# Third stage, selective scan: the terms of a tile summed by two VectorE reductions along the terms' axis in place of seven GpSimd additions

## What is computed

```python
x_ssm = silu(causal_depthwise_conv(x_ssm, conv_w, conv_b))
dt = softplus(x_ssm @ dt_w + dt_b)
Bm = x_ssm @ B_w          # 16 states
Cm = x_ssm @ C_w
A = -exp(log_A)
# for each token t, in order:
h = h * exp(min(dt_t * A, 0)) + (dt_t * x_t) * B_t
y_t = sum over states (h * C_t)
# then
y = y + x_ssm * D_param
y = (y * silu(z)) @ W_out
out = residual + y
```

## Time and profile before

| | us |
|---|---|
| median of the 3 runs | 1027.2 |
| the three runs | 1036.17, 1026.03, 1027.2 |
| the profiled execution, time | 1038.13 |
| the profiled execution, span of the core | 1036.3 |
| VectorE busy | 679.9 (66%) |
| TensorE matmuls busy | 860.4 (83%) |
| GpSimd busy | 457.0 (44%) |
| first and last multiplication of line 1139 start at | 529.5, 735.8 |

### The profile page before, as it was taken

The page is one execution under the profiler, slowest core; times in us unless marked ns, Lnnn a source line. Parts: engine busy times, 40 slices in busy tenths (PEclk is TensorE's granted clock), DMA queues, the critical chain, the costliest instruction groups (busy, mean ns, idle before and its releaser), DMA issues. The chain is left out here.

```text
span 1036.3 us, 21603 instructions
## 1 busy us (share of the span) xinstructions
PE 860.4 (83%) x8256; PEld 709.6 (68%) x8256; DVE 679.9 (66%) x1965; ACT 556.8 (54%) x1050; POOL 457.0 (44%) x781
## 2 busy tenths in 40 slices
PE   1888882669999999988777778987479999999994
PEld 1778771558888888866645556765358878888783
DVE  2687765665888888764279999999864181461712
ACT  1454551236676766646567787787355263552630
POOL 1486754222454545336357777776740020020201
PEclk9985665557899999888888888788679999999997
DMA  9100001100000000000000000000000000000000
GB/s 310 49 19 17 22 18 44 49 1 2 1 3 2 2 2 2 1 2 1 1 1 1 1 1 1 1 1 1 0 1 1 1 14 8 1 21 1 14 8 20
DMA packets 22149, 16.76 MB, mean 16 GB/s; under 512 B 2576, under 2 KB 20376, under 8 KB 21792
## 3 DMA queue, kind: packets, MB, share of 16 engines
q1 hardware_dynamic: 17408, 8.39, 2.9%
q10 hardware_dynamic: 4640, 7.01, 2.0%
HBM read 11.20 MB, written 4.19 MB: 15 GB/s over the span
## 5 line engine op out<-in xcount | busy, mean ns | idle before, releaser
L118 POOL TENSOR_TENSOR d_ln_ve<-d_ln_mv,eps 128x4 f32<-128x4 f32 x16 | 3.2, 201 | 228.7 <-DVE d_ln_mv L112 228.7
L1331 PE MATMUL ps<-h_h,wh_h 128*128 128x512 f32 x256 | 99.6, 389 | 0.0
L1333 PE MATMUL ps<-h_l,wh_h 128*128 128x512 f32 x256 | 99.6, 389 | 0.0
L1332 PE MATMUL ps<-h_h,wh_l 128*128 128x512 f32 x256 | 99.6, 389 | 0.0
L1410 PE MATMUL ps<-w_e,he 128*128 128x128 f32 x512 | 88.0, 312 | 3.2 <-ACT he L684 2.9
L684 ACT ACTIVATE he<-ps,pp 128x256 f32<-128x256 f32 x128 | 59.8, 472 | 43.5 <-PE ps L1333 38.0
L1344 PEld LDWEIGHTS ps<-mov,hbd 32*128 32x128 f32 x2048 | 82.1, 242 | 0.0
L1410 PEld LDWEIGHTS ps<-w_e,he 128*128 128x128 f32 x512 | 78.1, 224 | 5.4 <-ACT he L684 4.7
L1344 PE MATMUL ps<-mov,hbd 32*128 32x32 f32 (+1 forms) x2048 | 80.7, 317 | 0.0
L1298 DVE TENSOR_TENSOR d_y<-ps,w_s 128x512 f32<-128x512 f32 x8 | 5.5, 692 | 102.9 <-PE ps L1729 102.9
L1264 DVE TENSOR_TENSOR h_l<-hid,h_h 128x512 fp32r<-128x512 f32 x64 | 48.5, 772 | 31.2 <-ACT h_h L891 30.3
(11 more groups left out here) (255 smaller groups left out, 2610.8 us busy)
## 6 DMA issues: line engine op xcount, KB each, us to landing
x<-in_x SPq DMA_DIRECT2D x16, 128.0 KB
w_h<-in_w_h ACTq DMA_DIRECT2D x2, 1024.0 KB, 8.3
x<-x SPq DMA_DIRECT2D x16, 128.0 KB, 1.8
xB<-x SPq DMA_DIRECT2D x32, 64.0 KB
out_x<-xB SPq DMA_DIRECT2D x32, 64.0 KB
w_m<-in_w_m ACTq DMA_DIRECT2D x3, 256.0 KB, 5.5
xB<-in_w_e ACTq DMA_DIRECT2D x1, 512.0 KB
w_e<-in_w_e ACTq DMA_DIRECT2D x1, 512.0 KB
```

The source lines that it names most:

```text
L1331: pe.matmul(dst, a_h, b_h, start=start, stop=True, skip_group_check=True)
L1332: pe.matmul(dst, a_l, b_h, start=False, stop=True, skip_group_check=True)
L1333: return pe.matmul(dst, a_h, b_l, start=False, stop=True, skip_group_check=True)
```

## The change

Two new tiles per lane stand beside `term`: `ysum`, 32 chunks x 8 tokens, and `late`, 32 x 4. In `terms`, VectorE now raises a new semaphore `c_terms` with the second multiplication, waits for it, and issues two reductions: the first adds the four wide terms of each of the 256 tokens into `ysum`, the second the four thin ones into `late`, and the second raises `c_term`. `sums` is gone from GpSimd. `skips` gets one more addition, linked to the next, of `late` to the last four tokens of each chunk in `ysum` (128 elements), then adds `xd` and raises `c_ys` as before. `add_sums` reads `ysum`. All terms of a token are added now, where `sums` left out those that are zero.

```diff
--- before.py
+++ after.py
@@ -289,6 +289,8 @@
         hd = sb("hd", [P, DS, NB])
         hc = [sb(f"hc{l}", [P, DS, NCH]) for l in LANES]
         term = [sb(f"term{l}", [P, HALF * NCH * (CH + HALF)]) for l in LANES]
+        ysum = [sb(f"ysum{l}", [P, NCH, CH]) for l in LANES]
+        late = [sb(f"late{l}", [P, NCH, HALF]) for l in LANES]
         cbd = [sb(f"cbd{l}", [P, NT]) for l in LANES]
         hcT = [sb(f"hcT{l}", [P, 4, D]) for l in LANES]
         xd, yi, ya = (chan("c_" + n) for n in ("xd", "yi", "ya"))
@@ -330,7 +332,7 @@
             a_y a_zn a_z a_o a_x a_stored b_xn b_xb b_t_ps b_qk_ps b_v_ps b_kT b_hbd b_vT b_vbd b_s_ps b_sm b_ex
             b_pT b_m_ps b_ctx b_ctxt_ps b_msgT b_y b_y_ps b_zn b_h b_ht_ps b_hT b_hTl b_l_ps b_lg b_le b_hot b_hott_ps b_hotT b_on b_z b_o
             b_x c_xn_ c_t_ps c_xT_ c_in_ps c_zs_ c_xs_ c_dt_ps c_b_ps c_c_ps c_zb_ c_sp_
-            c_dt_ c_dec c_bcT c_prod c_g1_ps c_term c_ys c_xd c_cbd c_wall c_wt_ps c_u c_yi1 c_bbd c_xr c_br_ps c_wendT c_st_ps
+            c_dt_ c_dec c_bcT c_prod c_g1_ps c_terms c_term c_ys c_xd c_cbd c_wall c_wt_ps c_u c_yi1 c_bbd c_xr c_br_ps c_wendT c_st_ps
             c_hs c_hct_ps c_hcT c_yi_ps c_y c_out_ps c_o_ c_x d_xn_ d_t_ps d_xh d_xl d_y_ps d_o_ d_x d_stored""".split()
         S = {n: sem(n) for n in SEMS}
         he_ps, he_ready, e_done = (sem(n) for n in ("he_ps", "he_ready", "e_done"))
@@ -540,23 +542,14 @@
                 pool.tensor_tensor(c_ln1.nm[m][:, :], c_ln1.nm[m][:, :], minus[:, 0:2], ALU.mult
                                    ).then_inc(c_ln1.rstd_ready, 1)
 
-            def sums(t):
-                l = t % 2
+            def skips(t):
+                l = t % 2
+                pool.wait_ge(S["c_xd"], t + 1)
                 pool.wait_ge(S["c_term"], t + 1)
-                wide = term[l][:, 0:HALF * PAIR].rearrange("p (s c t) -> p s c t", s=HALF, t=CH)
-                thin = term[l][:, HALF * PAIR:].rearrange("p (s c t) -> p s c t", s=HALF, t=HALF)
-                y = wide[:, HALF - 1]
-                for j in range(1, HALF):
-                    chain.link(pool.tensor_tensor(y[:, :, j:CH], y[:, :, j:CH], wide[:, HALF - 1 - j, :, j:CH], ALU.add))
-                for j in range(HALF, CH):
-                    chain.link(pool.tensor_tensor(y[:, :, j:CH], y[:, :, j:CH], thin[:, CH - 1 - j, :, j - HALF:HALF],
-                                                  ALU.add))
-
-            def skips(t):
-                l = t % 2
-                pool.wait_ge(S["c_xd"], t + 1)
-                y = term[l][:, (HALF - 1) * PAIR:HALF * PAIR]
-                pool.tensor_tensor(y, y, xd[l][:, :], ALU.add).then_inc(S["c_ys"], 1)
+                y = ysum[l][:, :, HALF:CH]
+                chain.link(pool.tensor_tensor(y, y, late[l][:, :, :], ALU.add))
+                pool.tensor_tensor(flat3(ysum[l][:, :, :]), flat3(ysum[l][:, :, :]), xd[l][:, :], ALU.add
+                                   ).then_inc(S["c_ys"], 1)
 
             def stored(t):
                 pool.wait_ge(S["c_o_"], t + 1)
@@ -569,8 +562,6 @@
                     products(1)
                 if have(-2):
                     c_ln2.rstd_and_shift(pool, chain, eps, half, minus, (n - 2) % 4, n - 1)
-                if have(0):
-                    sums(n)
                 if have(4):
                     scales(n + 4)
                 if have(0):
@@ -1142,13 +1133,19 @@
                 dve.tensor_tensor(split(term[l][:, HALF * PAIR:].rearrange("p (s c t) -> p s c t", s=HALF, t=HALF)),
                                   split(w[:, 0:HALF, :, HALF:CH]),
                                   ps[:, PAIRS:PAIRS + 4, WIDE:BC_AT].rearrange("p g (s c t) -> p s g c t", s=HALF, t=HALF),
-                                  ALU.mult).then_inc(S["c_term"], 1)
+                                  ALU.mult).then_inc(S["c_terms"], 1)
+                dve.wait_ge(S["c_terms"], t + 1)
+                dve.tensor_reduce(flat3(ysum[l][:, :, :]), term[l][:, 0:HALF * PAIR].rearrange("p (s k) -> p k s", s=HALF),
+                                  AX.X, ALU.add)
+                dve.tensor_reduce(late[l][:, :, :].rearrange("p c t -> p (c t)"),
+                                  term[l][:, HALF * PAIR:].rearrange("p (s k) -> p k s", s=HALF), AX.X, ALU.add
+                                  ).then_inc(S["c_term"], 1)
 
             def add_sums(t):
                 l = t % 2
                 dve.wait_ge(S["c_ys"], t + 1)
                 dve.wait_ge(S["c_yi1"], t + 1)
-                chain.link(dve.tensor_tensor(yi[l][:, :], yi[l][:, :], term[l][:, (HALF - 1) * PAIR:HALF * PAIR], ALU.add))
+                chain.link(dve.tensor_tensor(yi[l][:, :], yi[l][:, :], flat3(ysum[l][:, :, :]), ALU.add))
 
             def gated(t):
                 l = t % 2
```

More of the change, by code:

```diff
@@ L541, in scales @@
                                    ).then_inc(c_ln1.rstd_ready, 1)
-            def sums(t):
-                l = t % 2
-                pool.wait_ge(S["c_term"], t + 1)
-                wide = term[l][:, 0:HALF * PAIR].rearrange("p (s c t) -> p s c t", s=HALF, t=CH)
-                thin = term[l][:, HALF * PAIR:].rearrange("p (s c t) -> p s c t", s=HALF, t=HALF)
-                y = wide[:, HALF - 1]
-                for j in range(1, HALF):
-                    chain.link(pool.tensor_tensor(y[:, :, j:CH], y[:, :, j:CH], wide[:, HALF - 1 - j, :, j:CH], ALU.add))
-                for j in range(HALF, CH):
-                    chain.link(pool.tensor_tensor(y[:, :, j:CH], y[:, :, j:CH], thin[:, CH - 1 - j, :, j - HALF:HALF],
-                                                  ALU.add))
             def skips(t):
@@ L557, in skips @@
                 pool.wait_ge(S["c_xd"], t + 1)
-                y = term[l][:, (HALF - 1) * PAIR:HALF * PAIR]
-                pool.tensor_tensor(y, y, xd[l][:, :], ALU.add).then_inc(S["c_ys"], 1)
+                pool.wait_ge(S["c_term"], t + 1)
+                y = ysum[l][:, :, HALF:CH]
+                chain.link(pool.tensor_tensor(y, y, late[l][:, :, :], ALU.add))
+                pool.tensor_tensor(flat3(ysum[l][:, :, :]), flat3(ysum[l][:, :, :]), xd[l][:, :], ALU.add
+                                   ).then_inc(S["c_ys"], 1)
             def stored(t):
```

## The result

The changed kernel takes 1061.9 us in the median of four runs (1059.1 to 1065.2), the kernel before 1030.6 (1026.0 to 1036.2). The ratio is 1.030, 95% interval 1.023 to 1.037: slower by 3%, about 31 us. The forecast was 1062. The profiled execution after has a span of 1063.1 us against 1036.3.

What follows compares the result with a forecast made beforehand. VectorE's own program was taken to bound the third stage: 48.8 us of strided reductions less 13.7 us given back make +35.1 on a median of 1027.2, so 1062 us; own range 1058 to 1074, whole range 1040 to 1076.

Steps and rivals of the forecast that it cites:

- The bound: Third stage: its length is VectorE's own program, 13.86 us a tile, so work put on VectorE counts in full.
- The reductions: VectorE's two added reductions and the wait on c_terms in terms: 3.05 us a tile with the stride, 48.8 us over 16.
- the full-rate rival: VectorE's new reductions run at one element a cycle wherever they read: 1.84 us a tile, +15.7, 1042.9 us; chance 22%.
- The give-back: VectorE's operations on two SBUF tiles speed up once GpSimd's seven additions are gone: 13.7 us less.
- The half that I gave to lines 1194 and 1108: Less sure recovery of these two VectorE operations from GpSimd's work: 4.1 us counted of 8.2.
- the part that I called sure: Lines 1163 and 1172 on VectorE, slowed beside GpSimd's additions, return to their fastest times: 9.6 us.
- The sum: Whole change: 48.8 us added on VectorE less 13.7 us returned, +35.1 us, 1062 us for the median.
- What was taken to cost nothing: c_term coming 3.05 us later, before pairs on TensorE and skips on GpSimd, was to cost no time.
- The clock rival: TensorE idles more in longer turns, its granted clock falls to 0.50 and its chain holds up VectorE: +47, 1074; chance 6%.
- The "not slower" rival: Reductions at full rate and VectorE regaining 32.1 us from GpSimd, line 1118 included: -2.7, 1024.5 us; chance 6%.

Runs made afterwards that it cites:

- The kernel with neighbours: The changed kernel with its two reductions reading four neighbouring elements per result instead of four lying 256 (128) apart, output not the reference's: 1043.3 us, ratio 1.010 to the kernel before.

## Why the prediction was right

**The bound.** Right. VectorE sets the turn before and after, and every microsecond of VectorE's own work counted once a tile.

**The reductions.** Counted 3.05 us a tile, 48.8 us. Measured between starts (620.13 - 619.41 = 0.72 for the second multiplication with the wait, then 622.93 - 620.13 = 2.80 for the two reductions, less the 0.60 that the multiplication had): 2.92 us, 46.7 us over 16. The reduction of 1024 took 1.938 us for 2.03 forecast, that of 512 took 1.031 for 1.08, since the stride cost 0.70 ns per element and not the 0.785 of line 1201. The kernel with neighbours shows that the stride is the whole difference from the full rate. There the full-rate rival's price held to the hundredth: in one turn its two reductions and the wait add 1.84 us (619.42 to 621.86, less 0.60). That the rival's 1042.9 us was met by 1043.3 is chance all the same: it stood for +15.7 us on a median of 1027.2, and the measured rise is 10.7. Of the two places of the Trainium skill, one fell and one held. The sentence of VectorE: DVE Perf Modes (Mode 1×) about "weird strides" at one result per cycle doesn't hold for fp32 in SBUF here (1.938 us against 1.220). The note on cachelines of SBUF — State Buffer (Door 1: The DMA port swizzle) has the direction right, and the size is from the runs: 0.70 ns per element read at strides of 128 and 256 elements, 0.79 written at a stride of 4.

**The give-back.** Counted 13.7 us, in the profiled execution it is larger: by busy time, step sizes 11.7 - 7.2 = 4.5 (counted 5.0), scan 15.8 - 10.8 = 5.0 (4.6), line 1194 12.8 - 10.3 = 2.5 and line 1108 (477 - 361) x 32 = 3.7 (4.1 for both), line 1118 0.1 (0), and the weighted input and line 1201, which were not counted, 1.8 and 0.5. Together 18.1 us, 4.4 more than counted. Two terms were mis-sized. The half that I gave to lines 1194 and 1108 came out at 6.2 us instead of 4.1, nearly all of line 1194's loss and two thirds of line 1108's. And the 2.3 us of the weighted input and line 1201 were put at nothing without a reason. The reading of line 1194 was also wrong: the prediction has it meet GpSimd's small operations, but in the kernel before it stands beside the seven additions themselves, which run to 617.21 in this turn, and in the changed one it mostly stands beside operations of two elements, too short to hold it up:

```profile
616.26 0.77 DVE L1194 TENSOR_TENSOR hd<-hc,dec 128x256 f32<-128x256 f32 x1
626.16 0.62 DVE L1191 TENSOR_TENSOR hd<-hc,dec 128x256 f32<-128x256 f32 x1
```

In all 16 tiles of the kernel before, line 1194 starts while one of the additions runs, and so does the weighted input in 15. Their loss belonged to the part that I called sure. Line 1108 (one turn of before, then of after, each with GpSimd's addition of the skip) came back because that addition now ends 0.04 us before it begins, and the products still wait for `bcT`:

```profile
619.99 0.72 POOL L559 TENSOR_TENSOR term<-term,c_xd 128x256 f32<-128x256 f32 x1
620.25 1.26 DVE L1108 TENSOR_SCALAR c_xq<-xB,c_ln_mv,c_rs 128x128 f32<-128x128 f32 x2
```

```profile
629.23 0.72 POOL L551 TENSOR_TENSOR ysum<-ysum,c_xd 128x256 f32<-128x256 f32 x1
629.99 0.57 DVE L1099 TENSOR_SCALAR c_xq<-xB,c_ln_mv,c_rs 128x128 f32<-128x128 f32 x2
```

This line reads one tile, and two values of each partition, and is held up all the same: two SBUF tiles are not the whole condition.

**The sum.** The two errors, 2.1 us too much for the reductions and 4.4 too little for the give-back, both made the forecast too long: 46.7 - 18.1 = 28.6, and with 1.7 us more idle time before the states' product 30.3 us. The body says 27.5 us for 15 turns, 29.3 for 16, and the runs 31.1. Forecast were 35.1 on a median of 1027.2; on the 1030.6 that the four runs of before have in the end, the forecast would have been 1065.7. That the median came out at the very microsecond is chance; the mechanism held, and each size within 5 us.

**What was taken to cost nothing.** The later `c_term` held up neither VectorE nor TensorE: `pairs` isn't among VectorE's waits, and TensorE's idle time before the turning of the states was still there (31.4 us in 14 turns). Only GpSimd's skip waited for it, in the last three tiles (12.6 us), where no `scales` stands ahead of it; it then ran beside the step sizes, 0.56 us there instead of 0.42. The clock rival didn't come: the body was granted 0.76 in the profiled execution after and 0.83 before, and what it can have cost VectorE is at most the 2.0 us before line 1118. The "not slower" rival asked for line 1118 to be given back; it stayed at 47.3 us to 47.4.

## What to carry to other kernels

An operation that is hidden in the list of waits can still cost the engine that sets the time: compare the fastest and the usual duration of that engine's instructions, and where they differ ask what another engine does at that moment. Before a sum is moved to VectorE, price its access pattern: a terms' axis that is outermost cost 0.7 ns per fp32 element read here, and laying it innermost cost as much in the writer. Give such work to the engine that has idle time in every turn and that the busy one doesn't wait for: TensorE took this sum in its gap of 2.3 us, and of all the kernels that compute the whole sum here only that one is faster than the kernel before (0.985).

## What the runs showed of the hardware

A stride in SBUF costs VectorE 0.7 to 0.8 ns per fp32 element: 0.70 ns read by a reduction at strides of 128 and 256 elements, 0.785 ns read by a multiplication at a stride of 8 (line 1201), 0.79 ns written by a multiplication at a stride of 4. The step sizes, an operation of VectorE with two SBUF inputs, ended 0.28 us behind the end of the GpSimd instruction that ran when they started, in 57 cases of 57, so one GpSimd addition of 512 elements (1.39 us) made a 0.42 us operation last 1.38 us. A reduction beside GpSimd went on undisturbed, at 1.95 against 1.94 us, while a `tensor_scalar` on one SBUF tile (line 1108) was held up: 0.54 to 0.55 us in the turns in which it starts 0.26 us behind the skip's addition, where it took 0.31 to 0.32 beside nothing. Cutting GpSimd's instructions in two lowered the step sizes from 0.73 to 0.52 us and the scan from 0.99 to 0.85, and moved other work of GpSimd's beside the multiplications, so that the time stayed the same (0.999).
